# A one-core adaLN block (gated linear attention, then a mixture of experts): another order and other engines in its first microseconds

## The reference, cut to what matters

```
x: (2, 1024, 256) tokens, c: (2, 256) conditioning vector, wmod: (256, 1536)
mod = silu(c) @ wmod                       # six rows of 256 per batch: sa, ca, ga, sb, cb, gb
h = layernorm(x) * (1 + ca) + sa
x = x + ga * attention(h)
h = layernorm(x) * (1 + cb) + sb
x = x + gb * moe(h)                        # 8 experts, top 2, and a shared expert

attention(h): q, k, v = h@Wq, h@Wk, h@Wv   # 16 heads of 16, chunks of 64 tokens
  gk = log_sigmoid(h @ Wg1 @ Wg2 + bg2)/16 # the low rank (16 wide), then the logits
  G  = cumsum of gk within a chunk
  o  = scores of a chunk (masked) @ v + (q * exp(G)) @ state;  state carried from chunk to chunk
  out = (rmsnorm(o) * norm_w * silu(h @ Wgate)) @ Wo           # Wgate: "the gate"
```

## Time and profile before

| | us |
|---|---|
| median of 3 runs | 379.55 |
| lowest and highest | 378.67, 379.7 |
| the profiled execution | 377.23 |
| its span | 375.5 |

### The profile page before, as it was taken

One profiled execution on the slowest core, in us unless ns is written; L12 is line 12 of the kernel. 1 busy time (PEld: TensorE's weight loads), 2 busy tenths in 40 slices (PEclk: granted clock), 3 DMA queues, 4 the chain that ended last, 5 costly groups with the idle time before them and its releaser, 6 DMA issues.

```text
span 375.5 us, 10003 instructions
## 1 busy us (share of the span) xinstructions
PE 360.4 (96%) x3871; PEld 226.3 (60%) x3872; DVE 238.5 (64%) x578; ACT 144.1 (38%) x303; POOL 147.2 (39%) x253
## 2 busy tenths in 40 slices
PE   8999999998999888999999999999999999999996
PEld 8445656564666465556844754766666666665464
DVE  4199576995799479846392772165555555556386
ACT  3697537817581612271052411114333333332110
POOL 7705007100710162025353075342667766675300
PEclk9999999999999999999999999999999999999999
DMA  7970200000000000069921082332333333311396
GB/s 209 328 243 17 101 4 3 2 3 4 2 2 5 2 2 4 3 189 294 313 68 57 1 195 87 103 105 73 111 96 104 102 99 92 99 57 44 97 351 232
DMA packets 29901, 36.66 MB, mean 98 GB/s; under 512 B 4567, under 2 KB 26530, under 8 KB 29860
## 3 DMA queue, kind: packets, MB, share of 16 engines
q1 hardware_dynamic: 26452, 27.58, 24.7%
q0 software_dynamic: 3408, 8.51, 6.8%
HBM read 23.31 MB, written 13.68 MB: 99 GB/s over the span
## 4 chain that ended last, share of the span: by engine, by line
PE 88%; DVE 5%; ACT 4%; issue 2%; DVEq 0%; POOL 0%; ACTq 0%; POOLq 0%
PE at_ps L1868 13%; PE work L1477 10%; PE at_ps L1477 8%; PE work L1526 6%; PE at_ps L1492 6%; PE work L1891 4%; PE work L1492 4%; PE at_ps L1526 3%; PE work L1893 3%; PE work L1667 3%; PE at_ps L1852 2%; PE at_ps L1699 2%; PE work L1717 2%; PE o_even L1620 2%; PE at_ps L1564 2%
## 5 line engine op out<-in xcount | busy, mean ns | idle before, releaser
L680 POOL DMA_INDIRECT ys_tokens<-er_pos,goal_u x39 | 42.1, 1080 | 33.5 <-DVE er_pos L1400 26.0
L1868 PE MATMUL at_ps<-arena 128*128 x156 | 54.5, 472 | 0.0
L651 POOL DMA_INDIRECT xs_sorted<-h2tok,pos_u x32 | 31.4, 982 | 38.2 <-DVE pos_u L1024 15.8
L609 POOL TENSOR_TENSOR sq<-sq,sg 128x512 f32<-128x512 f32 x8 | 10.0, 1273 | 89.5 <-issue 89.5
L1868 PEld LDWEIGHTS at_ps<-arena 128*128 128x128 f32 x156 | 26.6, 190 | 14.9 <-issue 6.6
L930 ACT ACTIVATE arena<-at_ps 128x176 f32<-128x176 f32 x39 | 12.4, 318 | 58.8 <-PE at_ps L1868 56.5
L1400 DVE SCALAR_TENSOR_TENSOR er_pos<-work,goal,sq 128x256 f32<-128x256 f32 x39 | 17.2, 479 | 22.0 <-PE work L1898 21.0
L1477 PE MATMUL work<-h2T,sup_sb 128*128 128x512 f32 x56 | 25.8, 600 | 1.3 <-ACT hs L701 1.3
L1380 DVE TENSOR_TENSOR arena<-at_ps,arena 128x176 f32<-128x176 f32 x39 | 13.3, 342 | 18.4 <-ACT arena L930 15.9
L1227 DVE COPY_PREDICATED arena<-causal,at_ps 128x512 f32<-128x512 uint32 x32 | 20.4, 719 | 4.0 <-PE at_ps L1564 4.0
L1492 PE MATMUL at_ps<-sdn_sb,hs 128*128 128x256 f32 x100 | 22.1, 380 | 0.0
(11 more groups left out here) (290 smaller groups left out, 823.0 us busy)
## 6 DMA issues: line engine op xcount, KB each, us to landing
h2tok<-xs_sorted SPq DMA_DIRECT2D x40, 131.5 KB
arena<-ys_tokens SPq DMA_DIRECT2D x8, 512.0 KB, 7.6
arena<-in_e_up SPq DMA_DIRECT2D x8, 352.0 KB
x_sb<-in_x SPq DMA_DIRECT2D x4, 512.0 KB, 9.2
out_rows<-x_sb SPq DMA_DIRECT2D x16, 128.0 KB, 4.1
sup_sb<-in_s_up SPq DMA_DIRECT2D x2, 640.0 KB, 4.7
xs_sorted<-state SPq DMA_DIRECT2D x2, 526.0 KB
xs_sorted<-state SPq DMA_DIRECT2D x8, 131.5 KB
```

The source lines that it names most:

```text
L651: g.indirect_dma_start(out=xs_dram, out_offset=bass.IndirectOffsetOnAxis(ap=pos_u[:, k, t:t + 1], axis=0), in_=h2tok[:, t, :], in_offset=N ...
L680: g.indirect_dma_start(out=ys_dram, out_offset=bass.IndirectOffsetOnAxis(ap=goal_u[:, i:i + 1], axis=0), in_=yout[:, q % 2, u, :], in_offs ...
L1868: ins = t_.matmul(at_ps[2 + u % 2][:, 0:2 * FE], xT[:, u % 2, k * P:(k + 1) * P], eup[:, bass.ds(e, 1), k, :].rearrange("p a n -> p (a n)" ...
```

## The change

Five edits, all in the first microseconds:

1. c is loaded by ScalarE's queue instead of SyncE's.
2. x of block 0 is loaded as two transfers of two tiles each; VectorE waits for the second one only ahead of the third tile's statistics.
3. There are 16 products of ones at the start instead of 14, and three more between `mod_cols` and the transposes. All of them write another bank (`o_odd` instead of `at_ps0`), since the transposes of block 0 now go to the banks of `at_ps0` and `at_ps1`.
4. The first half of block 0's `hT` is made by ScalarE as before, the second half by VectorE, each with a semaphore of its own (`ht_first`).
5. On TensorE the gate's first half is computed ahead of the low rank, its first product as soon as the first half of `hT` is there; the gate's second half is computed ahead of the logits Z instead of behind them.

```
-    units = [(("MODC", 0, 0), 2), (("XT", 0, 0), BANKS["XT", 0]), (("XT", 0, 1), BANKS["XT", 1])]
+    units = [(("MODC", 0, 0), 2), (("XT", 0, 0), 4), (("XT", 0, 1), 5)]
...
+    put("G", 0, 0)
     put("LR", 0, 0)
-    put("G", 0, 0)
+    put("G", 0, 1)
     put("Z", 0, 0)
     put("Z", 0, 1)
-    put("G", 0, 1)
...
         @block.sync
-            sp.dma_start(x_sb[:, 0:TPB, :], x[0:BLK, :].rearrange("(t p) c -> p t c", p=P)).then_inc(ld_x[0], 16)
-            sp.dma_start(csb[:, :, :], cT).then_inc(ld_c, 16)
+            for s, t0 in ((ld_x[0], 0), (ld_x_half, TPB // 2)):
+                sp.dma_start(x_sb[:, t0:t0 + TPB // 2, :],
+                             x[t0 * P:(t0 + TPB // 2) * P, :].rearrange("(t p) c -> p t c", p=P)).then_inc(s, 16)
...
         @block.scalar
+            act.dma_start(csb[:, :, :], cT).then_inc(ld_c, 16)
             act.wait_ge(ld_c, 16)
...
             act.wait_ge(modc_ready, 2)
-            evac_xT(0)
+            wait_unit(act, ("XT", 0, 0))
+            a.activation(hT[:, 0, :], bank(("XT", 0, 0))[:, :], ACT.Identity,
+                         bias=cols[:, 0, 0, 0:1], scale=cols[:, 1, 0, 0:1]).then_inc(ht_first[0], 1)
...
         @block.vector
+                    if tile0 + t == TPB // 2 and which == 0:
+                        dve.wait_ge(ld_x_half, 16)
...
+            dve.wait_ge(modc_ready, 2)
+            wait_unit(dve, ("XT", 0, 1))
+            v.tensor_scalar(hT[:, 1, :], bank(("XT", 0, 1))[:, :], cols[:, 1, 1, 0:1], cols[:, 0, 1, 0:1],
+                            ALU.mult, ALU.add).then_inc(ht_first[1], 1)
             dve.wait_ge(const_pool, 1)
             z_min(0)
...
         @block.tensor
             pe.wait_ge(ones_ready, 1)
-            idle_products(14)
+            idle_products(16)
             pe.wait_ge(ident_ready, 1)
             mod_cols()
+            idle_products(3)
             transpose_x(0)
             idle_products(3)
+            pe.wait_ge(ld_wgate, 16)
+            o = begin(("G", 0, 0))
+            for k in range(KC):
+                pe.wait_ge(ht_first[k], 1)
+                ins = t_.matmul(o[:, :], wgate_sb[:, k, 0:P], hT[:, k, :], start=(k == 0), stop=(k == KC - 1))
+            ins.then_inc(unit_full, 1)
             pe.wait_ge(ld_wg, 16 * (NPAIR + 3))
             low_rank(0)
-            pe.wait_ge(ld_wgate, 16)
-            project(("G", 0, 0), wgate_sb, 0, hT)
+            project(("G", 0, 1), wgate_sb, 1, hT)
             gate_logits(0)
-            project(("G", 0, 1), wgate_sb, 1, hT)
```

More of the change, by code:

```diff
@@ L70 @@
 MASK_ORDER = (2, 3, 0, 1)
-FIRST_BANKS = {("V", 0): 4, ("K", 0): 5, ("K", 1): 2}
+FIRST_BANKS = {("V", 0): 4, ("K", 0): 5, ("K", 1): 2, ("XT", 0): 4, ("XT", 1): 5}
 SECOND_BANKS = {("Q", 0): 2, ("Q", 1): 3}
@@ L341, in adaln_moe @@
         yout = er_pos[:, :, :].rearrange("p a (t c) -> p a t c", t=2)
+        ld_x_half = sem("ld_x_half")
         ld_x = [sem(f"ld_x{i}") for i in range(NBLK)]
@@ L350, in adaln_moe @@
         const_pool, ident_ready, zero_ready, kv_full = sem("const_pool"), sem("ident_ready"), sem("zero_ready"), sem("kv_full")
+        ht_first = [sem("ht_first0"), sem("ht_first1")]
         modf_ready, mod_stored, ld_rows = sem("modf_ready"), sem("mod_stored"), sem("ld_rows")
@@ L396, in released @@
                 "MODC": [(modc_ready, 2)],
-                "XT": [(ht_ready, 2 * blk + j + 1)],
+                "XT": [(ht_ready, 2 * blk + j - 1) if blk else (ht_first[j % KC], 1)],
                 "LR": [(tt_ready, blk + 1)],
@@ L1533, in idle_products @@
                 for _ in range(n):
-                    t_.matmul(at_ps[0][:, 0:P], ones[:, :], ones[:, :], start=True, stop=True)
+                    t_.matmul(o_ps[1][:, 0:P], ones[:, :], ones[:, :], start=True, stop=True)
             def mod_cols():
@@ L1679, in low_rank @@
             def low_rank(s):
-                pe.wait_ge(ht_ready, 2 * s + 2)
+                if s:
+                    pe.wait_ge(ht_ready, 2 * s)
                 o = begin(("LR", s, 0))
```

## The result

Over 22 runs each, the median went from 378.91 to 379.72 us; the ratio of the runs is 1.0039 (95% interval 1.0020 to 1.0058), which is 1.5 us, while the two medians alone differ by 0.8. The change makes the kernel slower, by 0.2 to 0.6%. The profiled execution took 379.40 us instead of 377.23, with a span of 377.6 us instead of 375.5; both had full clock.

What follows compares the result with a forecast made beforehand. TensorE, busy 360.4 of 375.5 us, was taken as the bound. Z's delay of +2.19 us (+0.95 products of ones, +1.24 order) less 0.16 reserve gave +2.03 on 379.55: 381.6 us, range 379.7 to 383.0.

Steps and rivals of the forecast that it cites:

- Rival A: Z's delay is given back or never arrives, leaving TensorE's own +0.37 us: 379.9 to 380.3, say 380.0; chance 0.14.
- Two more products at the start: TensorE's start: products of ones end at 7.08 instead of 6.63 us, so silu(c)'s products begin 0.28 us later.
- Silu(c)'s products: TensorE ahead of the transposes: from their start to the transposes they take 1.90 us, as before.
- Three more products in the middle: TensorE between silu(c)'s products and the transposes: six passes of 0.112 us, +0.67 us.
- The loads: x in halves and c on ScalarE's queue: xn earlier by 0 to about 1 us, but it waits; worth 0.
- Order: TensorE, gate's first half ahead of low rank, second ahead of Z: adds 1.24 us to Z's delay, Z starting at 16.15.
- VectorE's half of hT: Evacuation of block 0's second half: takes 0.64 to 0.69 us, in time for the gate's second product, cost 0.
- The reserve: ScalarE's idle 0.16 us at 28.56, ahead of the values' second part, absorbs that much of Z's delay.
- A sign that failed: TensorE's idle time ahead of block 1's low rank was to grow from 0.57 to more than 1.5 us.
- a wait that the prediction called covered: VectorE's queries times decay end at 30.85 us, ahead of ScalarE's need of their bank at 32.2.
- The forecast's chain over ScalarE and VectorE: From Z to block 1's low rank: as long as TensorE's stream, 0.16 us reserve, so Z's +2.19 arrives as +2.03.
- Rival B: TensorE from transposes to gate's second half: clock falls in plain runs, added products prevent 5 us loss, giving 377; chance 0.09.

Runs made afterwards that it cites:

- e7: e3's kernel with the logits Z placed between the two products of the gate's first half on TensorE; median 378.23 us, ratio to the kernel before 0.9984.
- e10: e7's kernel with three more products of ones between silu(c)'s products and the transposes, 14 at the start; median 378.80 us, ratio to the kernel before 1.0014.
- e2: The changed kernel with TensorE's old order (low rank, gate's first half, Z, gate's second half); median 378.24 us, ratio to the kernel before 1.0027.
- e4: The kernel before with only the five added products of ones (16 at the start, three in the middle); median 378.45 us, ratio 1.0018.
- e5: The changed kernel itself, run again beside the kernel before on the same chip; median 379.80 us, ratio 1.0036.
- e8: The changed kernel with four more products of ones behind Z, ahead of the values; median 380.26 us, ratio to the kernel before 1.0044.
- e9: e7's kernel with 16 products of ones at the start and none in the middle; median 376.64 us, ratio to the kernel before 0.9966.
- e11: e7's kernel with 16 products of ones at the start and three in the middle; median 378.02 us, ratio to the kernel before 1.0001.
- e3: The changed kernel without the five added products and with TensorE's old order, so loads and evacuation alone; median 378.45 us, ratio to the kernel before 1.0006.
- e6: The kernel before with only TensorE's order changed (gate's first half, low rank, gate's second half, Z); median 379.70 us, ratio 1.0038.
- e1: The changed kernel without the five added products of ones (14 at the start, none in the middle); median 379.44 us, ratio to the kernel before 1.0032.

## Why the prediction was right, and where its sizes were off

The time went the way forecast and lies in the stated range, but only just: the measured median of 379.72 stands at its lower edge of 379.7, and 1.9 us under the forecast time of 381.6. Rival A's 380.0 is nearer to it; it is the traces that decide for the forecast, not the time. Of the 1.9 us, 0.64 come from the base (379.55 was the median of three runs; over 22 runs it was 378.91), and the rest from a step of 0.8 us between the medians, 1.5 by the ratio, instead of 2.03. The two profiled executions differ by 2.17 us (379.40 against 377.23; 379.2 was forecast), but that agreement is in part luck: up to block 1's low rank the profile shows +1.51, which is 0.5 less than the forecast, and another 0.6 came behind it, where the forecast had nothing. Point by point:

- Two more products at the start: forecast +0.28 for silu(c)'s products, measured +0.04. Their last weight load ends at 6.84, not 7.08, because in this execution the products ran fast from an earlier moment on. wmod had landed by then (issued at 1.79, 4.9 us to land), so they, not wmod, set the start. This term of the sum was mis-sized: it took one profile's end of the 14 products as given. Over the profiles with 14 at the start their weight loads took 4.81 us (e7) to 6.05 (e10), a spread of 1.2 us, more than the 0.45 that two products are worth: this end does move from run to run, which one trace could not show. Behind 16 products TensorE still waited 0.4 to 0.8 us for wmod in five profiles (e2, e4, e5, e8, e9) and not at all in the changed kernel's and e11's.
- Silu(c)'s products took 1.78 us to the next weight load (8.55 - 6.77), not 1.90. With the term above this puts the transposes at +0.52 instead of +0.95.
- Three more products in the middle: +0.67 forecast, +0.67 measured (9.22 - 8.55; e10 to e7: 25.13 - 24.45 = 0.68).
- The loads: xn was ready at 8.1 instead of 8.65 and waited; worth 0, as said. e3's three full-clock runs agree.
- Order: Z starts 6.5 us behind the transposes' first weight load (15.75 against 9.22), forecast 16.15 - 9.65 = 6.50. Right. e2 shows that undoing it gives back 1.05 of the forecast 1.24 in the profile, e6 that the order without the second engine costs about 2.1 us at full clock.
- VectorE's half of hT: 0.81 us, forecast up to 0.69, in time for G0's second product.
- The reserve: 0.16 forecast, about 0.26 found (1.79 became 1.53 at the values' second part).
- A sign that failed: the idle time ahead of block 1's low rank was to grow from 0.57 to more than 1.5 us. It stayed at 0.58. TensorE waits earlier instead, 0.16 and 0.75 us ahead of its transposes, for VectorE's queries times decay, a wait that the prediction called covered. It looked only at ScalarE's need of their bank, and block 1's transposes on TensorE need it first.
- Rival A is refuted by e2 and e8. The forecast's chain over ScalarE and VectorE is shown.
- Rival B was half right. The clock does fall in plain runs, and with the added products fewer runs show it. I set it aside because the one trace had full clock everywhere; 79 of 105 runs have not. But it was 2.0 us that a fallen clock costs on average (378.9 - 376.9), not 5, and the products save it in 34 runs of 100 (13 of 22 at full clock instead of 26 of 105): 0.7 us. This term was missing from the sum.

Put together: the full-clock runs are 2.4 us slower (379.3 against 376.9), 0.7 is given back by the clock, and 1.7 is left, against a measured 1.5. The runs behind these means are from several chips, and on e5's the share rose more (7 of 12 against 4 of 35), so the tenths mean little.

Left open: of the 2.4 us at full clock the profile shows 1.5 up to block 1's low rank and 2.1 at the end. The 0.6 behind it can't be laid to the change. From the start of block 1's low rank to the span's end the kernel before takes 343.9 us and the changed one 344.5, but the same stretch takes 344.7 in e5, the same kernel, and in the other profiles with full clock throughout between 343.5 (e9) and 344.4 us, although TensorE's stream behind that point is the same in all. What moves it, and where the last 0.3 arise, stays open, and so does what makes the clock fall at the start.

The Trainium skill, TensorE: Matmul & The Clock Gate, Part 1, "What's actually happening", has the clock fall behind a whole stretch without work. In this part no profile here has TensorE without work for more than 1.01 us behind its first product, and the clock fell in e1, e3 and e6 all the same, so these traces do not agree. Ahead of each of the three falls stood a wait of 0.53 to 0.80 us and then products that stream 2 columns; but the same stood in e7, and in e4 with 16 products, and there the clock stayed full.

## What to carry to other kernels

Ask of every reordering which of two chains of equal length it lengthens: work moved ahead of the head of the other chain costs time there (1.05 us for the 1.91 of one gate half) and gains nothing on the busiest engine. Filler products are free where the engine waits for a transfer anyway, and there they went with more runs at full clock (e9); the same filler behind the transfer is paid in full (e10). And read the granted clock of many plain runs before taking a profile with full clock for the kernel's usual state.

## What the runs showed of the hardware

- The granted clock was 0.50 in stretches of the first 16 us in three of the six profiles of kernels with 14 products at the start (e1, e3, e6; not in before, e7, e10), in none of the eight profiles with more. It fell far behind as well, in stretches that all kernels share: between 128 and 132 us in e1 and between 88 and 94 us in e4. The page's row of e1:

```profile
PEclk9899999999999899999999999999999999999999
```

- The granted clock does not show the slow products at the very start. In the kernel before one weight load of the products of ones takes 333 ns up to about 5.9 us and 192 ns from then on, with a granted clock of 1.00 in both stretches; and the moment of this step moves, so that the weight loads of 14 such products took between 4.81 us (e7) and 6.05 us (e10).
- At half clock half of the time is lost work, but not all of that arrives at the end. In e3 the fall lasted 6.8 us, and block 1's low rank came 2.75 us later than in e7 behind silu(c)'s start (27.20 against 24.45). Part of the loss fell on waits: e7's 0.40 us ahead of the low rank is gone in e3.
- c on ScalarE's own queue let silu(c) run at 3.62 us instead of 4.56, 0.94 us earlier, with its issue of 0.44 us ahead of the first table load. Nothing waited for it.
